# One GNN kernel on one core: edge softmax and weighted node sums merged into one stage, weights stored by chunk, destinations read from the edge list

## The reference, cut to what matters

```
a = a @ aW3 + ab3                                   # [50000, 8]
alpha = jax.nn.softmax(a, axis=0)                   # over all edges
alpha_mean = alpha.mean(axis=1, keepdims=True)
agg = jax.ops.segment_sum(msg * alpha_mean, dst, num_segments=N)
```

## Time and profile before

| what | value |
|---|---|
| median of three runs | 5012.18 us |
| profiled execution, its own time | 5044.25 us |
| span of that execution | 5042.4 us |
| PE busy, share of the span | 75% |
| granted TensorE clock, mean | 0.853 |
| softmax phase, first to last instruction | 1224.0 to 1262 us |
| sums phase, first to last instruction | 1262.5 to 1390 us |

### The profile page before, as it was taken

The page is one execution under the profiler, slowest core; times in us unless marked ns, Lnnn a source line. Parts: engine busy times, 40 slices in busy tenths (PEclk is TensorE's granted clock), DMA queues, the critical chain, the costliest instruction groups (busy, mean ns, idle before and its releaser), DMA issues. The chain is left out here.

```text
span 5042.4 us, 83052 instructions
## 1 busy us (share of the span) xinstructions
PE 3763.8 (75%) x23281; PEld 2288.7 (45%) x23281; DVE 1851.4 (37%) x5399; ACT 1538.0 (31%) x3573; POOL 1837.9 (36%) x1815
## 2 busy tenths in 40 slices
PE   3788777875754787777477787766677777999998
PEld 1455555543542444444344444433444444555564
DVE  4444444444753333333223333332232222335223
ACT  2333333332232333333233333322222222313112
POOL 1333333331033555555245555435545553000000
PEclk7888788887976898988788989877888787999999
DMA  3344444444755333333344455434434443554223
GB/s 108 106 121 125 114 123 121 123 117 77 238 171 169 79 93 90 85 90 89 81 113 122 118 132 129 111 89 107 107 101 108 107 106 80 172 180 157 83 89 121
DMA packets 673822, 586.67 MB, mean 116 GB/s; under 512 B 379103, under 2 KB 527621, under 8 KB 672901
## 3 DMA queue, kind: packets, MB, share of 16 engines
q1 hardware_dynamic: 579886, 377.56, 26.6%
q0 software_dynamic: 77008, 200.24, 15.0%
q10 hardware_dynamic: 16768, 6.91, 0.5%
HBM read 471.65 MB, written 112.79 MB: 116 GB/s over the span
## 5 line engine op out<-in xcount | busy, mean ns | idle before, releaser
L1967 POOL DMA_INDIRECT aw_y<-s_lrows,aw_src x1350 | 1379.7, 1022 | 1284.6 <-PE ps L2034 689.4
L2034 PE MATMUL ps<-aw_y,aw_pT 128*63 128x277 f32 x2700 | 481.8, 501 | 331.8 <-ACT aw_pT L2218 202.9
L742 POOL DMA_INDIRECT em_gs<-s_rows,em_idx x400 | 385.0, 963 | 699.3 <-DMA em_idx<-in_sd 539.0
L2943 PE MATMUL ps<-nl_adj,nl_table 126*128 126x504 bf16 (+1 forms) x3150 | 631.8, 357 | 2.3 <-DVE nl_table L3178 2.3
L1994 PE MATMUL ps<-ident,aw_y 128*128 128x128 f32 x2700 | 454.6, 308 | 188.3 <-DVE aw_y L2330 82.3
L2204 ACT ACTIVATE aw_yT<-ps 128x512 f32<-128x512 f32 x675 | 386.0, 597 | 365.3 <-remote 174.1
L1994 PEld LDWEIGHTS ps<-ident,aw_y 128*128 128x128 f32 x2700 | 344.4, 158 | 336.2 <-issue 177.9
L2018 PE MATMUL ps<-aw_yT,aw_qt 128*63 128x384 f32 x1800 | 372.0, 520 | 158.3 <-ACT aw_yT L2204 111.6
L2365 DVE COPY aw_axd<-ps 128x252 f32<-128x252 f32 x225 | 94.7, 421 | 1071.4 <-PE ps L2051 583.1
L2034 PEld LDWEIGHTS ps<-aw_y,aw_pT 128*63 128x63 f32 x2700 | 211.1, 165 | 524.2 <-issue 248.0
L2943 PEld LDWEIGHTS ps<-nl_adj,nl_table 126*128 126x128 bf16 x3150 | 301.9, 96 | 299.3 <-issue 6.1
(11 more groups left out here) (374 smaller groups left out, 6089.5 us busy)
## 6 DMA issues: line engine op xcount, KB each, us to landing
nl_adj<-s_adj SPq DMA_DIRECT2D x20, 3100.8 KB
aw_geoS<-s_geoS SPq DMA_DIRECT2D x450, 94.5 KB
nl_adj<-s_adj SPq DMA_DIRECT2D x15, 2325.6 KB
ws_msg<-s_msg SPq DMA_DIRECT2D x75, 384.0 KB, 3.9
aw_qt<-s_qt SPq DMA_DIRECT2D x225, 126.0 KB
s_msg<-em_msg SPq DMA_DIRECT2D x100, 256.0 KB
aw_y<-s_lrows,aw_src POOLq DMA_INDIRECT x1350
s_adj<-em_adj SPq DMA_DIRECT2D x75, 258.4 KB
```

The source lines that it names most:

```text
L742: pool.indirect_dma_start(out=gs[:, u, j, :], out_offset=None, in_=d["rows0"], in_offset=bass.IndirectOffsetOnAxis(ap=idx[:, u, 2 * j:2 * ...
L1967: pool.indirect_dma_start(out=y[:, u, j, 0:W], out_offset=None, in_=table, in_offset=bass.IndirectOffsetOnAxis(ap=src[:, u, j:j + 1], axis ...
L2034: m = nc.tensor.matmul(k.ps[64 * v:64 * v + HW, SUM, 0:SW], pT[:, SLOT[u], j, 64 * v:64 * v + HW], y[:, u, v * TH + j, 0:SW], start=j == 0 ...
L2943: m = nc.tensor.matmul(k.ps[:, bank(i, p), 0:cols * WN], source[:, p, q, b, :], adj[:, a % 2, 0:cols, b * WN:(b + 1) * WN], start=b == 0 a ...
```

## The change

The two phases become one (`weighted_sums`).

- The weights of 400 x 128 edges are turned on PE (four transposes), copied by ACT into chunk order (100 partitions x 512) and stored to HBM alone (`d["alpha"]`), as 100 rows of 2 KB. The pair of weight and destination is stored on the general path only.
- Each window loads three things, all from SP: the messages, its piece of the edge list (`ends`, source and destination as integers, 6 KB) and its weights (`share`, 3 KB). ACT issues no loads any more. The weights have a `value_load` of their own.
- There are 15 buffers for what is loaded and loops of 15 windows (`UM`), where there were 5. SP issues the first 15 windows' messages and ends before it clears semaphores and before the weights exist.
- DVE makes `sel` in one instruction from the integers and a table of bases; `dl` and the base's step are gone.

```diff
+    U, LAG, R, UM = 5, 2, 64 + WN, 15
...
+        ends = sb("ends", [128, UM, T, 2], I32)
+        share = sb("share", [128, UM, T])
+        msg = sb("msg", [128, UM, T * D])
+        base = sb("base", [128, NW])
...
+        pe_ = Steps(sem("pe"), ["AGG", "DEG"], UM)
...
         @block.sync
         def _(sp):
+            def load(w, u):
+                at = sp.value_load(k.starts[0:1, bass.ds(w * V, 1)], min_val=0, max_val=E)
+                sp.wait_ge(pe_.sem, pe_.of(w - UM, "DEG"))
+                sp.dma_start(msg[:, u, :], d["msg"][bass.ds(at, S), :]...).then_inc(msg_in[u], 16)
+                sp.dma_start(ends[:, u, :, :]..., d["sd"][bass.ds(at, S), :]...).then_inc(msg_in[u], 16)
+
+            def load_share(w, u):
+                at = sp.value_load(k.starts[0:1, bass.ds(w * V, 1)], min_val=0, max_val=E)
+                sp.dma_start(share[:, u, :], d["alpha"][bass.ds(at, S)]...).then_inc(share_in[u], 16)
+
+            with fits(sp):
+                for u in range(UM):
+                    load(u, u)
             k.clear_old(sp)
+            with fits(sp):
+                sp.wait_ge(chunk_ok, 4)
+                sp.dma_start(d["alpha"]..., by_chunk[:, :, :]...).then_inc(weight_out, 16)
+                sp.wait_ge(weight_out, 16)
+                for u in range(UM):
+                    load_share(u, u)
+                with sp.Fori(1, NW // UM) as i:
+                    for u in range(UM):
+                        load(UM * i + u, u)
+                        load_share(UM * i + u, u)
...
         @block.gpsimd
         def _(pool):
-            pool.memset(base[:, :], 0.0).then_inc(made, 1)
+            pool.affine_select(out=last, ...).then_inc(masked, 1)
+            pool.wait_ge(soft, 1)
+            pool.partition_all_reduce(most[:, :], part[:, :], 128, RMAX).then_inc(pooled, 1)
+            pool.iota(base[:, :], pattern=[[WN, NW]], ...).then_inc(made, 1)
             pool.memset(one[:, :], 1.0).then_inc(made, 1)
+            pool.wait_ge(soft, 3)
+            pool.partition_all_reduce(total[:, :], part2[:, :], 128, RADD).then_inc(pooled, 1)
...
                 def select(w, u, i):
-                    dve.wait_ge(pair_in[u], (i + 1) * 16)
-                    dve.wait_ge(s, of(w - 1, "BASE"))
-                    nc.vector.tensor_scalar(dl[:, u, :], pair[:, u, :, 1], base[:, 0:1],
-                                            None, ALU.subtract).then_inc(s, 1)
...
+                    dve.wait_ge(msg_in[u], (i + 1) * 32)
+                    dve.wait_ge(pe_.sem, pe_.of(w - U, "DEG"))
+                    nc.vector.scalar_tensor_tensor(sel[:, u % U, :, :], bc(k.iota_wn[:, :].unsqueeze(1), [128, T, WN]),
+                                                   base[:, bass.ds(w, 1)], bc(ends[:, u, :, 1:2], [128, T, WN]), ALU.add, ALU.is_equal).then_inc(s, 1)
...
+                    dve.wait_ge(share_in[u], (i + 1) * 16)
+                    nc.vector.tensor_tensor(wsel[:, u % U, :, :], sel[:, u % U, :, :], bc(share[:, u, :]...), ALU.mult).then_inc(s, 1)
-                    nc.vector.tensor_scalar(base[:, :], base[:, :], float(WN), None, ALU.add).then_inc(s, 1)
...
             pe.wait_ge(made, 2)
             pe.wait_ge(cleared, 1)
+            with fits(pe):
                 pe_.prime(pe)
                 turned.prime(pe)
+                pe.wait_ge(soft, 7)
+                for j in range(4):
+                    m = nc.tensor.transpose(k.ps[0:NC, U, j * 128:(j + 1) * 128], weight[:, :]..., k.ident[:, :])
+                m.then_inc(weight_turned, 1)
+                pe.wait_ge(chunk_ok, 4)
...
         @block.scalar
         def _(act):
-            def load(w, u):
...
+                act.wait_ge(weight_turned, 1)
+                for j in range(4):
+                    nc.scalar.activation(by_chunk[:, :, j], k.ps[0:NC, U, j * 128:(j + 1) * 128], ACT.Copy).then_inc(chunk_ok, 1)
```

More of the change, by code:

```diff
@@ L1038, in _ @@
[L1038 to L1070, removed]
@@ L1074, in window_sums @@
[L1074 to L1083, removed]
+        weight = sb("weight", [128, ns])
+        by_chunk = sb("by_chunk", [NC, 128, 4])
+        ends = sb("ends", [128, UM, T, 2], I32)
+        share = sb("share", [128, UM, T])
+        msg = sb("msg", [128, UM, T * D])
@@ L1119, in _ @@
             nc.vector.memset(k.ps[32:64, 0:U, 0:D], 0.0).then_inc(cleared, 1)
-            with dve.If(dve.value_load(k.fits[0:1, 0:1], min_val=0, max_val=1) == 1):
+            dve.wait_ge(masked, 1)
+            nc.vector.tensor_reduce(part[:, :], by_head, AX.X, ALU.max).then_inc(soft, 1)
+            dve.wait_ge(pooled, 1)
+            nc.vector.tensor_tensor(flat, flat, bc(most[:, :].unsqueeze(1), [128, ns, AH]), ALU.subtract).then_inc(soft, 1)
+            dve.wait_ge(exped, 1)
+            nc.vector.tensor_reduce(part2[:, :], by_head, AX.X, ALU.add).then_inc(soft, 1)
+            dve.wait_ge(pooled, 2)
+            nc.vector.reciprocal(inv[:, :], total[:, :]).then_inc(soft, 1)
+            dve.wait_ge(soft, 4)
+            nc.vector.tensor_scalar(part[:, :], inv[:, :], 1.0 / AH, None, ALU.mult).then_inc(soft, 1)
+            dve.wait_ge(soft, 5)
+            nc.vector.tensor_tensor(flat, flat, bc(part[:, :].unsqueeze(1), [128, ns, AH]), ALU.mult).then_inc(soft, 1)
+            dve.wait_ge(soft, 6)
+            nc.vector.tensor_reduce(weight[:, :], flat, AX.X, ALU.add).then_inc(soft, 1)
+            with dve.If(dve.value_load(k.fits[0:1, 0:1], min_val=0, max_val=1) == 0):
+                dve.wait_ge(soft, 7)
+                nc.vector.tensor_copy(pairs[:, :, 0], weight[:, :]).then_inc(soft, 1)
+            with fits(dve):
                 dve_.prime(dve)
@@ L1169, in sums @@
                 for j in range(T):
[L1170 removed]
+                    m = nc.tensor.matmul(k.ps[0:1, u % U, D:D + WN], one[:, :], sel[:, u % U, j, :], start=j == 0, stop=j == T - 1)
                 m.then_inc(pe_.sem, 1)
@@ L1207, in copy @@
                 act.sem_inc(hop["act"], 1)
-                nc.scalar.activation(rows[:, u, :], k.ps[0:R, u, 0:D], ACT.Copy).then_inc(act_.sem, 1)
-                nc.scalar.activation(deg[:, bass.ds(w * WN, WN)], k.ps[0:1, u, D:D + WN], ACT.Copy).then_inc(act_.sem, 1)
-            with act.If(act.value_load(k.fits[0:1, 0:1], min_val=0, max_val=1) == 1):
-                act_.prime(act)
-                for u in range(U):
-                    load(u, u)
-                with act.Fori(0, NW // U - 1) as i:
-                    for u in range(U):
-                        copy(U * i + u, u)
-                        load(U * i + u + U, u)
-                for u in range(U):
-                    copy(NW - U + u, u)
-                act.wait_ge(act_.sem, act_.of(NW - 1, "DEG"))
+                nc.scalar.activation(rows[:, u % U, :], k.ps[0:R, u % U, 0:D], ACT.Copy).then_inc(act_.sem, 1)
@@ new lines, in copy @@
+                nc.scalar.activation(deg[:, bass.ds(w * WN, WN)], k.ps[0:1, u % U, D:D + WN], ACT.Copy).then_inc(act_.sem, 1)
+            act.wait_ge(soft, 2)
+            nc.scalar.activation(flat, flat, ACT.Exp).then_inc(exped, 1)
+            with fits(act):
+                act_.prime(act)
+                act.wait_ge(weight_turned, 1)
+                for j in range(4):
+                    nc.scalar.activation(by_chunk[:, :, j], k.ps[0:NC, U, j * 128:(j + 1) * 128], ACT.Copy).then_inc(chunk_ok, 1)
+                with act.Fori(0, NW // UM) as i:
+                    for u in range(UM):
+                        copy(UM * i + u, u)
+                act.wait_ge(act_.sem, act_.of(NW - 1, "DEG"))
@@ new lines, in _ @@
+            with act.If(act.value_load(k.fits[0:1, 0:1], min_val=0, max_val=1) == 0):
+                act.dma_start(dst[:, :].rearrange("p (c j) -> p c j", j=4),
+                              d["dst"][0:EP].rearrange("(c p j) -> p c j", p=128, j=4)).then_inc(dst_in, 16)
+                act.wait_ge(dst_in, 16)
+                nc.scalar.activation(pairs[:, :, 1], dst[:, :], ACT.Copy).then_inc(dst_ok, 1)
+                act.wait_ge(dst_ok, 1)
+                act.wait_ge(soft, 8)
+                act.dma_start(d["pair"][0:EP, :].rearrange("(c p j) s -> p c (j s)", p=128, j=4),
+                              pairs[:, :, :].rearrange("p (c j) s -> p c (j s)", j=4)).then_inc(out, 16)
+                act.wait_ge(out, 16)
```

88 lines of the change are left out of this document (36 added, 52 removed).

## The result

The changed kernel takes 5098.06 us (median of four runs, 5088.23 to 5114.01). The kernel before, on the same chip, takes 4999.01 (four runs, 4978.45 to 5027.13). The ratio is 1.0188, with a 95% interval of 1.0146 to 1.0231: slower by more than 1%, as forecast (whether it is 2% stays undecided). The time lies inside the range, 22 us above the predicted one. The profiled execution took 5088.5 us (5086.7 of span, mean granted clock 0.843).

What follows compares the result with a forecast made beforehand. Before, a dependent chain, then PE and DVE together, set the time; after, SP's issuing would. Last weighted table 61.8 us later plus 2.1 at the end made +64 on 5012.18: 5076 us, range 5035 to 5108.

Steps and rivals of the forecast that it cites:

- The bound: Window loop: SP's issuing of loads sets the pace after the change, at 2.82 us a window against 1.6 before.
- Rival A: Window loop: PE, not SP, sets the pace, so the kernel is not slower, 4996 us; chance 0.06.
- The price of a window: SP's issue time for one window's three loads in the loop: 2.82 us, bounds 2.39 and 3.07.
- messages: SP's register load and DMA for a window's messages in the loop: 1.26 us, as before.
- ends: SP's second DMA in a window, for its piece of the edge list: 0.48 us.
- weights: SP's load of a window's weights in the loop, with its own register load: 1.08 us.
- Rival B: Window loop: SP's register loads stretch to 0.45 us, adding 22 us, 5098 us in all; chance 0.08.
- The start: Softmax to first product: first message load at 1233.0, first product at 1264.6 instead of 1268.04, 3.4 us gained.
- a turn of the early loads: Before the weights' store, SP issues messages and ends for each of 15 windows: 1.55 us each.
- the later strand: Before the weights' store, SP finishes at 1258.9, 4 us after the weights are ready, so the store waits for SP.
- Rival C: Early message loads begin with the phase, so all that follows is 4 us earlier, 5072 us; chance 0.06.
- The sum: Whole kernel: 61.8 us to the last weighted table plus 2.1 for clearing more semaphores, +64 us in all.

Runs made afterwards that it cites:

- e2: The changed kernel with the weights of windows 15 to 74 loaded from ACT's queue instead of SP's; 5015.72 us, ratio 1.0044 to the kernel before.
- e4: The kernel before with only the pairs' loads moved from ACT to SP, with their own register load; 5055.46 us, ratio 1.0102.
- e1: The changed kernel with POOL's table of bases and column of ones made ahead of its wait for the first DVE reduction; 5072.43 us, ratio 1.0140.

## Why the prediction was right, and where it was off

**The bound.** Right: SP's issue time sets the loop. It never waits there, e2 takes away 1.08 us of it and 62 us of the stage go, and e4 brings about the same into the old kernel alone. Rival A (SP not the pace, 4996 us) needed a turn under 1.49 us; it is 2.85.

**The price of a window.** 2.82 forecast, 2.85 for most turns, 2.93 as a mean. The terms hold one by one: messages 1.26 (1.26), ends 0.52 (0.48), weights 1.07 (1.08). What lies between 2.85 and 2.93 are ten slow turns: three of 3.4 to 3.6 us where the loop of 15 windows starts over, the others 3.0 to 3.5 us, such as the one of 1293.20 to 1296.70 in which the ends' DMA took 0.98 us to issue instead of 0.33. That makes 175.5 us where 169.2 were forecast, 6.3 more in the loop. Rival B (the register load stretches) is refuted, though its price, 5098 us, is by chance the measured median: the two register loads of a window have a median of 273 ns over the 75 windows.

```profile
L1055 SPq TENSOR_LOAD <-starts x75: 267/273/278, 1217.0 to 1450.6; - x75
L1062 SPq TENSOR_LOAD <-starts x75: 268/273/437, 1261.3 to 1452.3; - x75
```

(Columns: ns minimum, median, maximum.) The 600 ns of the Trainium skill's page "DMA: Bandwidth & Descriptors", section "Latency and other measured facts", would have made the loop 40 us longer still, by the estimate in the prediction; 273 ns decides.

**The start.** This is the step that was mis-sized. The prediction put the first message load 9.0 us into the stage, for `made` behind the reduction plus 0.4 us for a small table; the 7.05 us ahead of the first IOTA, which the trace of the kernel before shows, were not looked for. It came at 15.3: the small steps were done 7.3 us behind the reduction's end, not 0.4; the reduction itself came 0.3 sooner than I took, and from `made` to the load it was 1.1 instead of 1.3. From there the terms hold: a turn of the early loads 1.61 (1.55; the first took 2.11), 37 clears 2.1 us from first to last, the store 27.1 us behind the first load (25.9), landed 2.6 us after its issue (2.6). The first product came 4.0 us later than before, where 3.4 earlier was forecast. That SP, not the weights, is the later strand was right, and by more than thought: ACT's copies (its timeline) were done at 1246.6, 12 us ahead of the store:

```profile
1245.57 1.07 ACT L1210 ACTIVATE ws_by_chunk<-ps 100x128 f32<-100x128 f32 x4 [15.84 <-PE ps L1185]
```

Rival C (the loads begin with the phase) is refuted for the change; but its price, 4 us, was far too low, because that mistake hides in it too. e1 makes C true, and it is worth 11.5.

**The sum.** From the start of the stage to the last weighted table 238.9 us against 162.1: +76.8, where +61.8 was forecast; 7.4 of the difference is the start, and 7.6 lies between the first product and the last table, 6.3 of it in SP's 60 turns. Behind it 9.8 us against 7.9: +1.9, forecast 2.1. The next phase takes 4 us more, which I did not foresee and did not try; its cause is open. So +83 in the traces against +64. The medians moved by 86 against the 5012.18 that the prediction started from; 99 and 105 in the two comparisons. That the time lies only 22 us above the forecast is in part luck: the median of three from which it started lies 13 us above the 4999.01 of all four runs.

**What was said of the profile after.** Groups of three loads without waits, first product (1264.4, said 1265) and store (1258.7, said 1259) came out, the absolute places with help of the 7.6 us by which this execution was ahead. Wrong: PE isn't idle half of the loop but 26% of it, since its clock fell to the lower level. The prediction bounded that at 2.76 us a window, under SP's 2.82, and so it stayed hidden. And DVE's weighted table was released by the weights in 3 waits alone; the select ahead of it waits for the ends.

## What to carry to other kernels

Count the turn of the queue that issues, not only busy engines: instructions that read a register or issue a DMA are in no busy time, and the earlier trace rows told more of this change than all shares of PE and DVE. A DMA on the same register cost 0.5 us here, one with a register load of its own 1.1; where a loop's turn is near that sum, give the load to a queue that has room, or load one wider table. Before a small step is put behind a reduction over partitions on POOL, look in the trace for what the queue does ahead of that kind of step, and raise the semaphores that others prime on first.

## What was not expected of the hardware

- An IOTA on POOL right behind the reduction over partitions stood idle for 7.03 us, with two MODIFY_POOL_CONFIG of 108 ns at the head of the gap. Ahead of the reduction the same IOTA and MEMSET took 0.3 us with no gap (e1), and the reduction was not late by it. In the changed kernel such a pair stands wherever POOL goes from the one to the other: ahead of the first reduction (1216.9), of the IOTA (1223.2) and of the second reduction (1230.8). In e1 (1207.8) and in the kernel before (1224.6) it stands ahead of the first reduction alone, where the wait for DVE hides it; the MEMSET that follows the second reduction in the kernel before (1262.55) has none. The Trainium skill, "GPSIMD Engine Reference", section "Instruction dispatch", has about 6 us for the first call to newly loaded code of that engine, counted from MODIFY_POOL_CONFIG. The gap here, behind the same instruction, is 1 us longer; that it is the same cost no run shows.
- PE at the lower clock level for most of the loop (granted 0.55, 12 products in 1.51 us) cost nothing while loads came every 2.85 us; with loads every 1.77 us (e2) the granted clock was 0.95 with no edit on PE.
- Moving a load to another queue let the DMAs run at a share of 0.82 and 217 GB/s instead of 0.50 and 135: the DMA engines had room all along.
